# A decoder kernel on one core: GpSimd, which forms the inverse deviations, also normalises the tiles of the three attention chains, and the order of the chains is planned anew

## The reference

```python
def _layernorm(x, axis=-1, eps=1e-05):
    m = jnp.mean(x, axis=axis, keepdims=True)
    v = jnp.var(x, axis=axis, keepdims=True)
    return (x - m) / jnp.sqrt(v + eps)
...
x = _layernorm(x + _L1_attn_ref(x, L1_attn_W_qkv), axis=-1)
x = _layernorm(x + _L1_xattn_ref(x, ctx_1024, ctx_1024, ...), axis=-1)
x = _layernorm(x + _L1_ffn_ref(x, L1_ffn_scores, ...), axis=-1)
x = _layernorm(x + _L2_attn_ref(x, L2_attn_W_in, ..., L2_attn_decay, L2_attn_mix), axis=-1)
```

## Time and profile before

| | us |
|---|---|
| three runs | 927.79, 928.20, 923.42 (median 927.79) |
| the profiled execution, its own time | 925.06 |
| its span in the trace | 923.3 |
| busy in the span: PE, DVE, ACT, POOL | 774.0 (84%), 588.4 (64%), 472.5 (51%), 353.3 (38%) |
| chain 0, from the first product of a0 to the last tile of x0 | about 63.5 to 127.5 |
| chain 1 | about 350 to 565 |
| chain 2 | about 663.5 to 787 |

### The profile page before, as it was taken

The page is one execution under the profiler, slowest core; times in us unless marked ns, Lnnn a source line. Parts: engine busy times, 40 slices in busy tenths (PEclk is TensorE's granted clock), DMA queues, the critical chain, the costliest instruction groups (busy, mean ns, idle before and its releaser), DMA issues.

```text
span 923.3 us, 21465 instructions
## 1 busy us (share of the span) xinstructions
PE 774.0 (84%) x8139; PEld 551.1 (60%) x8139; DVE 588.4 (64%) x1573; ACT 472.5 (51%) x1094; POOL 353.3 (38%) x508
## 2 busy tenths in 40 slices
PE   5787968788998877999979997399289998899996
PEld 2465735565667765777447775155156676477665
DVE  4866958988897738988389883223178797211212
ACT  2114645677778655776337663044067574333341
POOL 3338713432444224444168750300566574000101
PEclk8877977999999998999969995689699899799999
DMA  8024000000000000000170000301745200000000
GB/s 310 1 77 174 2 2 1 1 2 1 2 1 2 1 2 1 3 3 3 39 236 3 3 3 1 88 27 35 222 136 169 65 2 3 0 1 1 1 12 12
DMA packets 31426, 37.98 MB, mean 41 GB/s; under 512 B 2912, under 2 KB 22624, under 8 KB 30816
## 3 DMA queue, kind: packets, MB, share of 16 engines
q1 hardware_dynamic: 30816, 35.58, 12.0%
q0 software_dynamic: 512, 1.05, 0.4%
HBM read 28.36 MB, written 8.26 MB: 40 GB/s over the span
## 4 chain that ended last, share of the span: by engine, by line
PE 48%; DVE 22%; issue 8%; POOL 7%; ACT 6%; DMA 4%; SPq 1%; DVEq 0%; POOLq 0%; ACTq 0%
PE bank L965 6%; PE bank L975 6%; PE bank L752 4%; PE bank L773 4%; PE bank L761 3%; PE bank L925 3%; DVE pairs L1476 2%; PE bank L788 2%; DVE pairs L1470 2%; DMA rel_scratch<-G 2%; PE bank L842 2%; POOL sm L1733 2%; DVE sm L1423 2%; POOL rstd L1705 1%; DVE mx L1426 1%
## 5 line engine op out<-in xcount | busy, mean ns | idle before, releaser
L1704 POOL TENSOR_SCALAR veps<-mv 128x1 f32<-128x1 f32 x112 | 29.4, 263 | 250.7 <-DVE mv L1361 250.4
L1733 POOL TENSOR_TENSOR sm<-sm,mx 128x512 f32<-128x512 f32 x80 | 84.0, 1053 | 43.8 <-DVE mx L1426 43.3
L1080 ACT COPY pT<-bank 128x512 f32<-128x512 f32 x112 | 65.5, 584 | 36.7 <-PE bank L761 35.3
L1075 ACT ACTIVATE pr<-sm 128x512 f32<-128x512 f32 x112 | 70.3, 632 | 25.4 <-POOL sm L1733 23.8
L761 PE MATMUL bank<-W,pr 128*128 128x128 f32 x448 | 72.5, 286 | 9.2 <-ACT pT L1080 7.3
L1643 DVE SCALAR_TENSOR_TENSOR XB<-bank,QM,XB 128x128 f32<-128x128 f32 x64 | 18.0, 344 | 92.3 <-PE bank L975 92.3
L1728 POOL TENSOR_TENSOR pairs<-KS,quad 128x512 f32<-128x512 f32 x56 | 60.0, 1073 | 27.8 <-ACT KS L1057 27.6
L752 PE MATMUL bank<-pairs,Q 64*128 64x256 f32 x448 | 68.6, 427 | 2.1 <-DVE sm L1411 1.0
L1705 POOL TENSOR_TENSOR rstd<-veps,W 128x1 f32<-128x1 f32 x112 | 64.2, 573 | 9.3
L773 PEld LDWEIGHTS bank<-VX,pT 64*64 64x64 f32 x3584 | 59.8, 139 | 11.9 <-issue 6.0
L965 PE MATMUL bank<-XT,big 128*128 128x512 f32 x128 | 64.2, 628 | 2.2 <-ACT G L1219 2.2
(11 more groups left out here) (292 smaller groups left out, 1879.9 us busy)
## 6 DMA issues: line engine op xcount, KB each, us to landing
big<-gup SPq DMA_DIRECT2D x4, 1024.0 KB, 8.8
rel_scratch<-G SPq DMA_DIRECT2D x16, 256.0 KB, 2.9
W<-small SPq DMA_DIRECT2D x1, 3206.5 KB, 12.0
big<-early SPq DMA_DIRECT2D x2, 1557.0 KB, 8.4
big<-down SPq DMA_DIRECT2D x8, 256.0 KB, 8.6
big<-e3w SPq DMA_DIRECT2D x2, 1024.0 KB
...
```

What stands on the lines that cost most here:

```text
L1075: act.activation(pr[:, u % 2, 4 * h:4 * h + 4, :, :].rearrange("p g b k -> p b g k"), sm[:, 2 * (u % 2) + h, :].rearrange("p (b g k) -> p ...
L1080: act.copy(pT[:, u % 2, 4 * h:4 * h + 4, :], bank[BK[f"tu{h}"]][:, :].rearrange("p (h n) -> p h n", h=4)).then_inc(pt_ready, 1)
L1733: tt(v, v, bc(mx[:, slot, :], [P, 8, S], 2), ALU.subtract).then_inc(pcentered, 1)
```

## The change

The step dve.fi becomes pool.fi. VectorE writes the sum and its statistics as before, GpSimd forms the inverse deviation and then, as a later instruction of its own stream, makes the normalised tile. VectorE now only counts the signals, so that it knows when a slot of `res` may be written again (`norm_ahead`). The last normalisation of the program, in `top2_ffn`, stays with VectorE, and so does the one inside `first_ffn`. No product, exponential or DMA is added or removed: 88 instructions leave VectorE's stream in the chains and 88 come into GpSimd's.

```diff
@@ VectorE, chain
+                def norm_ahead(name, t):
+                    norm_at[t % 4] = x_at[t] = due(x_ready)
+                    due(rstd_ready)
+                    if name != "x0":
+                        xt_at[t] = due(xt_ready)
...
                         stats(out_, t)
-                    if step == "fi":
-                        if name == "gelu" and t >= NT:
-                            dve.wait_ge(xt_ready, xt_at[t])
-                        finish(X[:, t, :] if name == "gelu" and t >= NT else res[:, t % 4, :], t)
-                        if name != "x0":
-                            xt_at[t] = due(xt_ready)
+                        norm_ahead(name, t)
@@ GpSimd, chain
                     if step == "rs":
                         rstds(t)
+                    if step == "fi":
+                        src = X[:, t, :] if name == "gelu" and t >= NT else res[:, t % 4, :]
...
+                        pool.wait_ge(rstd_ready, rstd_at[t % 4])
+                        ts(X[:, t, :], src, mv[:, t % 4, 0:1], rstd[:, t % 4, :], ALU.subtract, ALU.mult).then_inc(x_ready, 1)
@@ the planner's numbers (a few of some 60)
-            "pe.va": 0.95, "dve.on": 0.8, "pe.fo": 0.2, "act.o": 0.3, "pe.y": 0.5, "dve.re": 0.95, "pool.rs": 0.9,
-            "dve.fi": 0.2, "pe.x": 0.25, "act.x": 0.3, "pool.xb": 0.4, ...
+            "pe.va": 0.9, "dve.on": 0.65, "pe.fo": 0.15, "act.o": 0.2, "pe.y": 0.55, "dve.re": 0.9, "pool.rs": 0.57,
+            "pool.fi": 0.45, "pe.x": 0.2, "act.x": 0.2, "pool.xb": 0.46, ...
-AFTER_PE, AFTER, SAME = 0.35, 0.2, 0.05
+AFTER_PE, AFTER, SAME = 0.4, 0.25, 0.05
```

More of the change, by code:

```diff
@@ L152, in local_plan @@
     return out
-CHAIN_US = {"pe.k": 0.36, "act.k": 0.3, "pool.kv": 1.05, "pe.v": 0.36, "dve.v": 0.4, "pe.q": 0.36, "act.q": 0.92, "pe.rel": 1.0, "act.rel": 1.3,
-            "dma.rel": 6.0, "pe.sc": 0.95, "dve.sc": 1.4, "pool.ce": 1.05, "act.ex": 0.65, "pe.tu": 0.5, "act.pt": 0.6,
-            "pe.va": 0.95, "dve.on": 0.8, "pe.fo": 0.2, "act.o": 0.3, "pe.y": 0.5, "dve.re": 0.95, "pool.rs": 0.9,
-            "dve.fi": 0.2, "pe.x": 0.25, "act.x": 0.3, "pool.xb": 0.4, "dve.mix": 0.75, "pe.in": 0.36, "act.in": 0.4,
+CHAIN_US = {"pe.k": 0.28, "act.k": 0.3, "pool.kv": 1.02, "pe.v": 0.28, "dve.v": 0.28, "pe.q": 0.28, "act.q": 0.75, "pe.rel": 1.0, "act.rel": 1.3,
+            "dma.rel": 6.0, "pe.sc": 0.9, "dve.sc": 1.42, "pool.ce": 1.03, "act.ex": 0.55, "pe.tu": 0.49, "act.pt": 0.48,
+            "pe.va": 0.9, "dve.on": 0.65, "pe.fo": 0.15, "act.o": 0.2, "pe.y": 0.55, "dve.re": 0.9, "pool.rs": 0.57,
+            "pool.fi": 0.45, "pe.x": 0.2, "act.x": 0.2, "pool.xb": 0.46, "dve.mix": 0.6, "pe.in": 0.36, "act.in": 0.4,
             "dve.scan": 0.45, "pe.up": 0.65, "act.up": 0.65, "pe.dn": 0.65, "act.out": 0.65}
-CHAIN_BANK = {"k": 4, "v": 2, "q": 4, "tu0": 3, "tu1": 3, "va0": 6, "va1": 2, "fo": 5, "y": 7, "x": 5, "in": 2, "up0":
-              7, "up1": 3, "dn": 4}
-CHAIN_RANK = {"pe.sc": -4.0, "pe.v": 2.5, "pe.tu": -2.5, "pe.rel": -3.5, "dve.mix": 3.5, "act.ex": 4.0, "pe.va": 3.0,
-              "pe.y": 2.0, "pe.x": 3.5, "dve.re": 3.5, "pool.xb": 2.5, "dve.on": 2.0, "act.k": -4.0, "act.o": 3.5,
-              "dve.v": -2.5, "pe.up": -2.5, "pool.ce": -3.5, "act.pt": -1.0, "pe.fo": -2.5, "act.up": 4.0, "act.rel":
-              2.5, "pe.in": 3.0, "act.in": 0.5, "pool.kv": -1.5, "act.q": -1.0}
+CHAIN_BANK = {"k": 4, "v": 2, "q": 4, "tu0": 3, "tu1": 3, "va0": 6, "va1": 2, "fo": 5, "y": 7, "x": 5, "in": 3, "up0":
+              6, "up1": 3, "dn": 4}
+CHAIN_RANK = {"pe.sc": -4.0, "pe.v": 3.5, "pe.tu": -2.5, "pe.rel": -1.0, "dve.mix": 2.5, "act.ex": 3.5, "pe.va": 3.0,
+              "pe.y": 2.0, "pe.x": 3.5, "dve.re": 3.5, "dve.on": 2.0, "act.k": -3.5, "act.o": 2.0, "dve.v": -2.5,
+              "pe.fo": 1.0, "pool.kv": -1.0, "act.up": 1.5, "pool.fi": -1.5, "pe.k": -0.5, "pe.dn": 3.0, "dve.scan":
+              -3.0, "act.out": 0.5, "act.in": -2.0}
 STAGE_RANK, CHAIN_PATIENCE = 7, 0.02
@@ L251, in chain_plan @@
     for step, other, *depth in CHAIN_RINGS:
-        for x2 in (0, 1) if step in ("pe.v", "pe.va") else (None,):
+        for x2 in (0, 1) if step == "pe.v" else (None,):
             mine = [j for j in queue.get(step, []) if x2 is None or (stages[j[1]] == "x2") == x2]
-            past = queue.get({"ema.y": "pe.y", "a3.sc": "dve.sc"}.get(other, other), [])
+            past = queue.get({"ema.y": "pe.y", "att.y": "pe.y", "a3.sc": "dve.sc"}.get(other, other), [])
             past = [j for j in past if x2 is None or (stages[j[1]] == "x2") == x2]
+            if other == "att.y":
+                past = [j for j in past if stages[j[1]] in ATT]
             if other in ("ema.y", "a3.sc"):
@@ L261, in chain_plan @@
             for j in mine:
-                n += 1 if step == "pe.tu" and j[4] == 0 or step != "pe.tu" and not (step == "pe.va" and x2 and j[3]) else 0
+                n += 1 if step == "pe.tu" and j[4] == 0 or step != "pe.tu" and not (step == "pe.va" and j[3]) else 0
                 if 0 <= n - depth[x2 or 0] < len(past):
@@ L1700, in _ @@
             pool.wait_ge(masks_in, 16 * 9)
+            rstd_at = {}
             def rstds(t):
@@ L1705, in rstds @@
                 tt(rstd[:, t % 4, :], veps[:, t % 4, :], power, ALU.pow).then_inc(rstd_ready, 1)
+                rstd_at[t % 4] = due(rstd_ready)
             def chain(part):
@@ L1710, in chain @@
                 first = due.now(x_ready)
+                xt_at = {}
                 for step, name, u, t, s_, h in planned[part]["pool"]:
@@ L1735, in chain @@
                         rstds(t)
+                    if step == "fi":
+                        src = X[:, t, :] if name == "gelu" and t >= NT else res[:, t % 4, :]
+                        if name == "gelu" and t >= NT:
+                            pool.wait_ge(xt_ready, xt_at[t])
+                        if name != "x0":
+                            xt_at[t] = due(xt_ready)
+                        pool.wait_ge(rstd_ready, rstd_at[t % 4])
+                        ts(X[:, t, :], src, mv[:, t % 4, 0:1], rstd[:, t % 4, :], ALU.subtract, ALU.mult).then_inc(x_ready, 1)
                 due(x_ready, MT * len(normed))
```

12 lines of the change are left out of this document (7 added, 5 removed).

## The result

The changed kernel takes 945.23 us (median of 4 runs, 943.28 to 947.27), the kernel before 928.0 beside it: ratio 1.0174, 95% interval 1.0139 to 1.0209. It is slower by 17 us. The forecast was 922.5, the range 914 to 931, and slower had a chance of 0.12: wrong in sign and outside the range.

A forecast was written before the change was run, and what follows sets the result against it. TensorE's path was taken as the bound, with 43 us of gaps in which it waits for VectorE or, close behind, GpSimd. Seven terms summed to -2.9 us from 925.06, giving 922.2; the forecast was 922.5, range 914 to 931.

The forecast's parts named there:

- The price: One normalisation on GpSimd was taken to cost 0.55 us, with ends of 0.41 and 1.02.
- rival of the dear fi: Slower: a normalisation on GpSimd costs 1.02 us instead of 0.55, adding 13 us, time 935; chance 0.13.
- (a): Chain 0: GpSimd's queue, with 12 normalisations added and hardly any idle time, loses 1 us: +1.0.
- (c): From gelu to x2: nine normalisations on GpSimd delay x2's first scores, less TensorE's progress meanwhile: +3.2 us.
- (e): Ramp of a3: two normalisations on GpSimd delay the first scores, while VectorE's holds go: +1.0 us, up to +3.
- (g): Ends of the three chains: the last tile's normalisation takes longer on GpSimd: +0.7 us.
- (b): Ramp of a1 and what follows: VectorE is the bound and is relieved: -2.5 us, between 0 and -4.5.
- (d): From 472 to 552 us: VectorE's relief closes half of TensorE's gaps: -3.5 us, between 0 and -6.
- (f): From 700 to 775 us, x3: VectorE's relief closes two thirds of TensorE's gaps: -2.8 us, between 0 and -4.3.
- holds of about 1.05 us: VectorE's normalisations held until GpSimd's running instruction ends, seen in the ramp of a3 and x3, were to disappear.
- rival of no gain: TensorE's gaps come from latencies and its own order, so VectorE's relief gives half: 926.6 us; chance 0.31.
- case of 0.18: Larger gain: planner numbers nearer the rows let the order close a third of TensorE's gaps: 911 us; chance 0.18.

The follow-up runs named there:

- e3: Changed kernel with GpSimd's normalisation replaced by a multiplication by a constant, so its values are not the reference's: 942.7 us, ratio 1.0170.
- e12: Kernel before, with an equal normalisation into a scrap tile added on GpSimd after each of 88 reciprocal deviations, VectorE still doing the real one: 941.0 us, ratio 1.0155.
- e10: Kernel before, its plan kept row for row, only the normalisations moved from VectorE's list to GpSimd's: 939.1 us, ratio 1.0104.
- e9: Changed kernel, its plan kept row for row, only the normalisations put back from GpSimd's list into VectorE's: 942.0 us, ratio 1.0134.
- e13: Kernel before, with the 8 products of x0's bias and the token mask formed by ScalarE instead of GpSimd: 922.6 us, ratio 0.9924.
- e5: Changed kernel with chain 0 alone as in the kernel before (its plan and VectorE's normalisation): 938.9 us, ratio 1.0084.
- e7: Changed kernel with four extra, unused matmuls on TensorE ahead of its wait for each of the 8 gelu tiles: 955.3 us, ratio 1.0261.
- e11: Changed kernel without GpSimd's 8 products of x0's bias with the token mask in chain 0 (computation left out): 940.3 us, ratio 1.0134.
- e4: Changed kernel planned anew with the profile's prices, 0.8 for GpSimd's normalisation and 0.85 for the inverse deviation: 956.8 us, ratio 1.0308.
- e1: Changed kernel's planner numbers, banks and rings, planned anew with the normalisation left on VectorE: 962.5 us, ratio 1.0356.
- e2: Normalisation on GpSimd as in the change, but planned with all planner numbers, rules and banks of the kernel before: 963.9 us, ratio 1.0391.
- e16: Kernel before, planned anew with two assumed waits raised to 0.4 and 0.25 us; values no longer the reference's: 948.4 us, ratio 1.0179.

## Why the prediction was wrong

**The price** was inside its ends but not at my value: 0.81 against 0.55. By my own rival of the dear fi (13 us for 0.47 us more) this gives 922.2 + 7.2 = 929. That is still 16 us below the result, and e3, with my price, stands at 942.7. The size of this term was off, but it isn't the step that failed. With it the load side of the sum, (a), (c), (e) and (g), is 5.9 + 7.2 = 13.1 us, and e12, which has the load alone, measures 14 (7 to 22).

The estimate of 0.7 us from the Trainium skill, "GPSIMD Engine Reference", section "Engine selection", was nearer than my pick, and its advice to keep elementwise work on VectorE holds here: the move by itself cost 10 to 12 us (e10). Its remark that work with one input is roughly at the line rate does not hold for this form: 0.808 us at the median on GpSimd against 0.346 on VectorE. The form with a constant took 0.563 in the mean (e3), and no run has it on VectorE.

**The step that failed is the relief of VectorE**, my (b), (d) and (f): -2.5, -3.5 and -2.8, together -8.8 us, as a share of VectorE's removed work in TensorE's gaps. e12 against e10 measures all three at once, the same load with and without the relief: 2 to 5 us by the times, with wide intervals. Why it can't be large stands in the trace of the kernel before. TensorE's waits from 472 to 552, by what ended them (total us, times, longest):

```profile
PE bank L761 <- ACT pT L1080: 3.0, 7, 0.8
PE bank L685 <- DVE X L1365: 1.8, 3, 0.7
PE bank L719 <- DVE G L1391: 0.9, 2, 0.6
PE bank L752 <- DVE sm L1423: 0.5, 1, 0.5
```

I had taken half of the 7.0 us of gaps for (d). But 3.8 us of them were ended by ScalarE, and VectorE's largest share, 1.8 us, is the wait for the normalised tile itself, which stays in the tile's way on whichever engine makes it. Only 1.4 us were ended by VectorE's other work. The same count gives 3.3 us for (b), from 346 to 372, and 1.9 for (f), from 700 to 775: 6.6 us in all, less than the 8.8 that I took. (The view names only the last one to release; what delayed that one is not in it.)

And (b) came out with the other sign: gelu's first rs, counted from the start of chain 1, is 5.6 us later in the changed kernel; the load alone makes that 3.5 (e12), the move alone 3 (e10), the order alone 8 (e9). I had read "VectorE works 23.44 of 26 us" as "TensorE waits for VectorE". But VectorE's own normalisation waited for rstd, and so for GpSimd, and e13 shows the other side: with 5 us less on GpSimd, VectorE works 18.43 of the 20 us in which it had 14.13. I saw a busy engine and didn't ask who fed it. Also the holds of about 1.05 us went, as forecast, without a gain to be seen: chain 2 is as long in e12, which keeps VectorE's normalisation beside a busier GpSimd, as in e10 (141.9 and 141.8).

(d) by itself is not settled for the changed kernel. From x2's first scores to top1's first product it takes 88.4 us, the kernel before 93.7, which is more than I had forecast. e5 and e7, with the same code, have 89.4 and 88.3, but e11, with the same code too, 93.2; and e10 and e12 have 93.2 and 93.3. A gain by VectorE's relief would show in e10 and not in e12.

My rival of no gain (0.31), that TensorE's gaps come from latencies and from its own order, was the nearest of the four on this step, but it still gave the relief half of its size and the load the same price.

**(a), chain 0, +1.0**: right mechanism, too small. With 0.81 my own row gives +4.1; measured is +5.9 in the changed kernel, 5.1 in e10. I had let the queue run almost without idle time, and 38.65 of 40 us is near to that; the missing 2 us are inside the scatter of this stage.

**(c), gelu to x2, +3.2**: right mechanism and place. At 0.81 it would be +5.5; the ladder grew by 7.2, in e10 by 6.4. Nine normalisations of 0.81, less the 0.5 that went, are 6.8 us, and the ten that stand in the ladder's 22.7 us 7.6. The 1.3 us that I took off for TensorE's progress meanwhile can't show in the ladder; behind it they would have to be part of the times from x2's first scores above, where e10 has 0.5 us less than before.

**(e), the ramp of a3, +1.0**: the last tile of top1 came 5.8 us later than before after the start of that stage, in e10, which has the move without the new order, 1.2: my size was that of the move, and the order made it five times as large. By the end of chain 2 it was given back: (e) and (f) together were -1.8, and chain 2 measured +0.1, with a scatter that could hide either.

**(g), the ends, +0.7**: as forecast in kind. At the end of chain 0 the tile is done 0.90 us after rstd in place of 0.39, three times 0.5 us.

**The order** is the second step that failed. I had costed it at nothing but for its places. It costs 12 us by itself (e9) and 7 on top of the move (1.0174 against 1.0104). The pieces then come near the result, each with its interval: 922.2, 7.2 for the price, 4 to 7 for relief that wasn't there, 7 for the order, 940 to 943 against 945. I had put a case of 0.18 on its bringing 14 us, with the argument that its numbers lie nearer to the rows. e4 shows how little that argument is worth: numbers nearer still lose another 12.

**Still open**: why the remade order is slower by itself, down to an instruction. Its largest pieces are placed (the start of gelu 8 us later in e9), not explained. The clock isn't cleared outside the ladder. The trace has TensorE at the lower level for 43.9 us of chain 1 in the kernel before and 48.2 in the changed one, but for 84.5, 73.5, 91.3 and 85.3 in e1, e2, e4 and e16, whose chain 1 is 20 to 30 us longer. In e1 it stays there from 497.0 to 534.5, and for a part of that TensorE is itself the bound, for it works almost without a pause:

```profile
516.15 2.08 PE L754 MATMUL bank<-pairs,Q 64*128 64x256 f32 x8
518.15 0.80 PE L730 MATMUL bank<-CT,mixed 128*128 128x128 f32 x2
518.74 1.06 PE L763 MATMUL bank<-W,pr 128*128 128x128 f32 x4
519.73 1.89 PE L775 MATMUL bank<-VX,pT 64*64 64x5 f32 x64
```

So in e1 a part of the long loss goes by the clock there; by how much, and why the clock stayed low, no run shows. In the ladder e7 took 20 us of the lower level out of chain 1 (27.7 in place of 48.2) and it was as long as before.
